# A transformer stage on one core: the sums of the exponentials taken by thirds of the queries

## The reference

```python
def local_attention(q, k, v):                    # w = 32, nw = n // w windows
    bk2, bv2 = (look(bk), look(bv))              # keys of the window before and of its own: 64
    mask = (it < jb) | (it > jb + w) | (jb == -1)
    sim = jnp.einsum('bhwie,bhwje->bhwij', bq, bk2) * QK_SCALE
    sim = jnp.where(mask, -jnp.finfo(sim.dtype).max, sim)
    attn = jax.nn.softmax(sim, -1)
    out = jnp.einsum('bhwij,bhwje->bhwie', attn, bv2)
    return out.reshape(b, h, n, d)
```

## Time and profile before

| | us |
|---|---|
| median of three runs | 4260.25 |
| lowest, highest | 4258.24, 4265.11 |
| the profiled execution | 4258.92 |
| its span, first to last instruction | 4257.1 |
| PE busy in the span | 3308.7 (78%) |
| DVE busy | 2398.8 (56%) |
| ACT busy | 2023.6 (48%) |
| POOL busy | 1092.0 (26%) |

### The profile page before, as it was taken

The page is one execution under the profiler, slowest core; times in us unless marked ns, Lnnn a source line. Parts: engine busy times, 40 slices in busy tenths (PEclk is TensorE's granted clock), DMA queues, the critical chain, the costliest instruction groups (busy, mean ns, idle before and its releaser), DMA issues. The chain is left out here.

```text
span 4257.1 us, 72810 instructions
## 1 busy us (share of the span) xinstructions
PE 3308.7 (78%) x23929; PEld 1802.4 (42%) x23929; DVE 2398.8 (56%) x3964; ACT 2023.6 (48%) x3421; POOL 1092.0 (26%) x989
## 2 busy tenths in 40 slices
PE   2554777884198229999739999999999999999997
PEld 1111553451133103333226655655655655655664
DVE  6998445546722327777665554555555455455553
ACT  0000446543022006666526666666666666666664
POOL 0001000000033011111124444533534433443541
PEclk6998779878599559999979999999999999999998
DMA  4000001002043621101221111111111111111111
GB/s 144 22 22 12 27 23 35 21 25 60 4 107 82 42 24 27 25 24 28 48 93 37 47 43 37 49 31 46 50 30 49 47 30 45 38 47 37 44 37 40
DMA packets 182733, 178.81 MB, mean 42 GB/s; under 512 B 113361, under 2 KB 120065, under 8 KB 178194
## 3 DMA queue, kind: packets, MB, share of 16 engines
q1 hardware_dynamic: 145106, 172.99, 15.5%
q10 hardware_dynamic: 37344, 1.97, 0.9%
HBM read 81.96 MB, written 26.67 MB: 26 GB/s over the span
## 5 line engine op out<-in xcount | busy, mean ns | idle before, releaser
L2246 POOL TENSOR_TENSOR tr_t<-tr_t 128x512 f32<-128x512 f32 x384 | 488.5, 1272 | 708.8 <-DVE tr_t L2090 708.8
L2253 POOL TENSOR_TENSOR tr_nq<-tr_t,tr_rn 128x512 f32<-128x512 f32 x384 | 392.1, 1042 | 413.5 <-ACT tr_rn L1986 413.5
L1465 DVE TENSOR_REDUCE attn_mp<-attn_ps 128x1 f32<-128x512 f32 (+3 forms) x660 | 395.5, 657 | 162.0 <-PE attn_ps L1316 86.6
L1951 ACT ACTIVATE tr_pr<-tr_ps 128x768 f32<-128x768 f32 x264 | 213.5, 809 | 396.3 <-PE tr_ps L1773 395.2
L2089 DVE TENSOR_TENSOR tr_t<-tr_ps,tr_tab 128x512 f32<-128x512 f32 x384 | 263.5, 686 | 243.5 <-ACT tr_sq L1960 243.4
L2099 DVE TENSOR_TENSOR tr_o<-tr_ps,tr_rd 128x384 f32<-128x384 f32 (+1 forms) x264 | 144.1, 546 | 450.4 <-ACT tr_rd L1976 449.4
L1788 PE MATMUL tr_ps<-tr_w,tr_xs 128*128 128x512 f32 x768 | 371.2, 605 | 29.1 <-DVE tr_xs L2117 24.8
L1427 ACT ACTIVATE attn_pr<-attn_ps 128x768 f32<-128x768 f32 (+2 forms) x352 | 300.3, 870 | 167.7 <-PE attn_ps L1349 165.5
L540 ACT ACTIVATE att_pr<-att_ps 128x1024 f32<-128x1024 f32 x256 | 251.7, 1022 | 127.5 <-DVE att_ps L585 127.2
L1773 PE MATMUL tr_ps<-tr_qT,tr_kT 64*128 64x96 f32 (+1 forms) x4224 | 303.5, 283 | 7.9 <-issue 7.9
L317 PE MATMUL max_scores<-max_kh,max_qh 128*128 128x512 bf16 x512 | 155.7, 388 | 187.4 <-DVE max_mcol L358 131.3
(11 more groups left out here) (269 smaller groups left out, 5401.4 us busy)
## 6 DMA issues: line engine op xcount, KB each, us to landing
tr_v<-tr_va SPq DMA_DIRECT2D x144, 192.0 KB, 2.5
tr_v<-tr_va SPq DMA_DIRECT2D x144, 128.0 KB, 2.4
moe_cb<-scratch_combineT SPq DMA_DIRECT2D x32, 512.0 KB
tr_w<-in_w_half SPq DMA_DIRECT2D x12, 1024.0 KB
tr_v<-tr_va SPq DMA_DIRECT2D x48, 256.0 KB, 2.5
att_kh<-scratch_kp SPq DMA_DIRECT2D x34, 294.0 KB
scratch_kp<-proj_parts SPq DMA_DIRECT2D x36, 256.0 KB
tr_v<-tr_va SPq DMA_DIRECT2D x96, 64.0 KB, 2.2
```

The source lines that it names most:

```text
L1465: dve.tensor_reduce(dst, src, AX.X, ALU.max).then_inc(maxed, 1)
L2246: pool.tensor_tensor(t12[:, slot, i, 0, :], t12[:, slot, i, 0, :], t12[:, slot, i, 1, :], ALU.add).then_inc(summed, 1)
L2253: pool.tensor_tensor(nq[:, slot, i, :].rearrange("p (h e) -> p h e", e=DH), t12[:, slot, i, 0, :].rearrange("p (h e) -> p h e", e=DH), rn[ ...
```

## The change

The sums are taken by thirds of the queries. The middle third of each tile (128 columns: four heads by 32 queries) is still added up over all 128 key rows in two column tiles of 128x64. The first third is added up over key rows 0 to 63 and the last third over key rows 64 to 127, each for even and odd heads, in four tiles of 64x64 of the array. Each pass streams 128 columns instead of 384, and there are six matmuls instead of two in a tile. The sums lie in the order of third 2, 1, 0: the last third in the last 128 columns of the bank NUM, which were free, and the others at the start of the bank DEN, so that the two halves of the rows write to different banks and one view, `dens`, takes in all 384 columns. The semaphore `den_done` goes: `invert` waits for `num_done`, the end of the weighing of the values. `outputs` reads `rd` by thirds in the reverse order.

```diff
+        THIRD = NPAIR * WIN
+        dens = ps[:].rearrange("p a b -> p (a b)")[:, DEN * CH - THIRD:DEN * CH + 2 * THIRD]
@@ weigh
-                for e in range(2):
-                    mm = pe.matmul(ps[e * DH:(e + 1) * DH, DEN, 0:NPAIR * QT], ones[:], pr[:, slot, e, :], start=True,
-                                   stop=True, tile_position=(0, e * DH), skip_group_check=True)
-                mm.then_inc(den_done, 1)
+                for third, rows in ((1, slice(0, P)), (0, slice(0, 2 * WIN)), (2, slice(P - 2 * WIN, P))):
+                    for e in range(2):
+                        weights = pr[rows, slot, e, :].rearrange("p (a c) -> p a c", c=QT)
+                        pe.matmul(dens[e * DH:(e + 1) * DH, (2 - third) * THIRD:(3 - third) * THIRD], ones[rows, :],
+                                  weights[:, :, third * WIN:(third + 1) * WIN], start=True, stop=True,
+                                  tile_position=(rows.start, e * DH), skip_group_check=True)
@@ invert
-                act.wait_ge(den_done, a + 1)
-                act.activation(rd[:], ps[:, DEN, 0:NPAIR * QT], ACT.Ln).then_inc(rd_log, 1)
+                act.wait_ge(num_done, a + 1)
+                act.activation(rd[:], dens, ACT.Ln).then_inc(rd_log, 1)
@@ outputs
-                dve.tensor_tensor(o[:, :, (s % 4) * QT:(s % 4) * QT + width],
-                                  ps[:, NUM, 0:NPAIR * QT].rearrange("p (a c) -> p a c", c=QT)[:, :, 0:width],
-                                  rd[:].rearrange("p (a c) -> p a c", c=QT)[:, :, 0:width],
+                thirds = width // WIN
+                dve.tensor_tensor(o[:, :, (s % 4) * QT:(s % 4) * QT + width].rearrange("p a (t c) -> p a t c", c=WIN),
+                                  ps[:, NUM, 0:NPAIR * QT].rearrange("p (a t c) -> p a t c", t=3, c=WIN)[:, :, 0:thirds, :],
+                                  rd[:].rearrange("p (t a c) -> p a t c", t=3, c=WIN)[:, :, ::-1, :][:, :, 0:thirds, :],
                                   ALU.mult).then_inc(o_ready, 1)
```

More of the change, by code:

```diff
@@ L1674, in stage_transformer @@
         v_tiled = [S_("v_tiled0"), S_("v_tiled1")]
-        den_done, num_done, rd_log, rd_ready, o_ready = (S_("den_done"), S_("num_done"), S_("rd_log"),
-                                                         S_("rd_ready"), S_("o_ready"))
+        num_done, rd_log, rd_ready, o_ready = S_("num_done"), S_("rd_log"), S_("rd_ready"), S_("o_ready")
         out_done, x_added = S_("out_done"), S_("x_added")
```

## The result

The changed kernel takes 4371.44 us (4365.27 to 4378.02, four runs) against 4262.68 us before in the same session: a ratio of 1.0256, 95% interval 1.0237 to 1.0274, or 109 us more. The forecast was 4354, 91 to 94 us more, slower; its range reached from 4300 to 4405. The profiled execution has a span of 4365.3 us.

A forecast was written before the change was run, and what follows sets the result against it. PE's stream was taken to bound most steps, ACT's copy chain about three of eleven. Waits behind L1974's later start, 60 us, plus 264 p = 34 us gave 94 us and 4354 us; range 4300 to 4405.

The forecast's parts named there:

- p: PE's loss per query-tile step from two more shape changes, each 0.10 to 0.13 us, against less streaming: 0.13 us taken.
- Charging p 264 times: PE's loss p counted in every query-tile step of the transformer stage: 264 p = 34 us for p = 0.13.
- s = 4 and s = 7: Query-tile steps in each run of eleven that end on ACT's copy of kT or qT: 0.65 + p longer.
- s = 0: Query-tile step where PE waits for qT and the last query tile is 64 wide: 0.45 + p longer.
- s = 6: A query-tile step without a wait: to grow by PE's own loss only, 0.1 to 0.16 us.
- s = 3 and s = 10: Query-tile steps (s = 3 without feed-forward work) where kT's copy has 0.26 us slack before L1795: 0.39 + p longer.
- s = 3 beside feed-forward work: Query-tile step with a square ahead of ACT's exponentials: L1974 0.17 + p late, taken without slack.
- s = 2 beside it: Query-tile step with feed-forward work, L1845 waiting for v's copy after 0.34 us ACT idle: 0.15 + p longer.
- two at a time: Rival: the sums' outer 64x64 tiles run only in pairs, p = 0.34, 150 us more, 4410; chance 0.12.
- Absorbed lateness: Rival: ACT's lateness is absorbed and only PE's stream counts, 34 us, 4294; chance, with partly absorbed, 0.13.
- Free changes of shape: Rival: PE's changes between half and full rows cost nothing, ACT's chain still does, 5 us, 4265; chance 0.04.
- The faster side: Rival: quarters run side by side without draining and L1974 loses nothing, 55 us less, 4205; chance 0.05.

The follow-up runs named there:

- e2: The kernel before with one edit, Ln waiting for the values' matmuls instead of the sums': 4357.33 us, ratio 1.0225.
- e1: The changed kernel's PE stream, but the sums signal den_done again and Ln reads the bank DEN alone, leaving out the last third: 4265.93 us, ratio 1.0007.
- e4: Against the kernel before: sums by thirds, each over all 128 key rows in two 128x64 column tiles, all in DEN, with den_done: 4254.22 us, ratio 0.9978.
- e3: The changed kernel with the outer thirds first and the middle last, Ln still waiting for the values, a PE semaphore increment taking the wait ahead: 4347.12 us, ratio 1.0193.
- e5: The changed kernel with eight bf16 filler matmuls on PE after the transposes of step s = 4: 4352.33 us, ratio 1.0207.
- e11: The kernel before with Ln waiting for the values and eight filler matmuls after the transposes of step s = 4: 4334.61 us, ratio 1.0173.
- e3b: Changed kernel with outer thirds first, middle last, the sums' signal, and Ln reading DEN alone, leaving out the last third: 4239.00 us, ratio 0.9942.
- e10: Version with the last third in bank X0, but where the sums waited for X0 all thirds go over 128 rows into DEN: 4244.26 us, ratio 0.9962.
- e6: Changed kernel with outer thirds first, middle last, the sums' signal den_done, and the last third in bank X0: 4257.73 us, ratio 0.999 to the kernel before.
- e9: The kernel before with eight semaphore increments on PE ahead of each tile's sums, no matmul more: 4298.86 us, ratio 1.008.

## Why the prediction was right, step by step

- **The way and the mechanism** held: most of the loss is in Ln's wait for the values (e2, 94 us). PE's longer stream alone costs next to nothing (e1, 3 us, which is some 15 less the gain at the returns), but behind that wait it adds 26 us: the steps sum to 69 us in e2 and to 95 in the changed kernel.
- **p, PE's own loss**: 0.103 us measured, 0.13 taken, inside 0.10 to 0.16. Both changes of shape cost 0.10, the dearer neighbour of 0.13 was no guide. e4, without the changes, lacks the price, and e3, with one fewer, has 0.15 less. The rule of the Trainium skill (TensorEngine Tiling (Array Packing), section Tiling Modes) that a change of mode drains the engine agrees with this, for 64x64 too.
- **Charging p 264 times** was right only because Ln hangs on the values, so that p passes through ACT's chain too. e1, where it doesn't, shows the price hidden in three or four steps of eleven.
- **Steps that take the whole lateness, and one without a wait**: s = 4 and s = 7 grew by 0.76 (0.78 forecast), s = 0 by 0.57 (0.58), s = 6 by 0.10.
- **s = 3 and s = 10**: 0.61 against 0.52. I had taken 0.05 for the handover from a copy to L1795. It is 0.15: e2 grew there by 0.51 of 0.66. In the earlier trace rows kT's copy and the next matmul lie 0.15 apart, and that was the row to take. This term was mis-sized by 0.10.
- **s = 3 beside feed-forward work**: 0.66 against 0.30. The step that failed is "the rotation behind it on DVE waits for the squares anyway": the squares were late themselves, and the centring behind the rotation carried that back to ACT.
- **s = 2 beside it**: 0.10 against 0.28; in the step itself all of the lateness fitted into the slack.
- That these errors cancel is luck: the steps as measured sum to 12 x (3.93 + 3.98) = 95 us against 94.
- **Not foreseen at all**: the clock falls behind the longer waits, about 20 us (19 in e5, 23 in e11), and about 10 us won at the returns of the loop. The two partly cancel, which is luck too. 95 + 22 - 10 is 107, near the 109 measured. This is most of the 15 us by which the forecast was low.
- **Rivals**: two at a time is out (the outer group takes 0.17 a pass of four). Absorbed lateness is out by e2. Free changes of shape are out by the narrow windows. The faster side was nearer than I gave it: with the sums' signal and one change less it exists (e3b, e10), as the mechanism that I had priced at 55 us. But it brings 17 to 23, some 9 of them at the returns of the loop.

## What to carry to other kernels

When an edit moves a signal later, price the chain behind the signal first: here a wait on the next matmul group cost 94 us (e2), while the changed matmuls alone cost 3 (e1) and some 26 behind that wait. The change had put a third of the sums into the bank of the values, and with it came that wait; with the third in another bank it wasn't needed (e6, e10). Price each change of the array's shape against the columns saved: with two changes more the sums took 0.05 us longer than before, and with one more 0.05 less. Put groups of one shape next to each other, and let the odd one stand where the shape changes anyway. And when a wait on PE grows, look at the granted clock behind it, in more than one kernel, since the falls don't come behind every wait.

## What the runs showed of the hardware that I had not expected

- In the changed kernel PE's clock fell from 2.4 to 1.2 GHz after waits of 2.05 and 2.2 us, in 11 of the 24 runs of eleven steps. Behind waits of 1.39 us, over six kernels, it fell in 11 of 78 cases, none of them in the kernel before. Filler matmuls, which cut the waits to some 0.75 to 0.9 us, removed the falls behind them (e5, e11).
- Four 64x64 matmuls in the four quarters of the array run together at the speed of one: a pass of 128 fp32 columns took 0.16 us with its exposed weight load, as the middle third's pair did.
- A change of the array's shape costs 0.10 us and an exposed weight load of 0.05 (narrow windows; e3 has one change less and 0.10 + 0.05 less a step), in a stream that otherwise hides its weight loads.
- Eight semaphore increments in PE's queue cost 0.125 us a step (e9), while one cost nothing that could be seen (e3).
- At a return of the loop PE stands still for 2.4 to 3.2 us, and in some kernels a second time for 1.1 to 2.8 us (before, e2, e11).
